# The third pair's cross product in two clusters of column tiles, its codes summed by GpSimd

## The chip, the core and the metric

The kernel runs on one core of one Trainium2 chip, with the core's engines TensorE (matrix products into PSUM), VectorE, ScalarE, GpSimd, and SyncE, which issues most of the DMA transfers. The metric is device time in microseconds, lower is better. Three runs of the kernel before gave 602.71, 602.85 and 603.24 us, median 602.85 us.

## The reference

`x` is 16 sequences of 64 rows by 1024. The layer is a cross product with a quantised context, a causal attention with 32 heads, and a dense layer with low-rank experts, each on the normalised row and added to `x`. Cut to what matters here:

```python
def fake_quant(x, scale, zp):
    q = clip(round(x / scale + zp), 0, 255)
    return (q - zp) * scale

x = x + matmul(fake_quant(layernorm(x)), fake_quant(ctx))     # ctx: (16, 1024, 1024)
h = layernorm(x)
q, k, v = split(h @ qkv_w + qkv_b)                            # rope on q and k, 32 heads of 32
x = x + softmax(rope(q) @ rope(k).T / sqrt(32) + causal) @ v @ out_w + out_b
x = x + layernorm(x) @ W.T + bias + sum_e w_e * (layernorm(x) @ A_e.T) @ Bf_e.T
```

The quantised product is worked out on integer codes: the product of the centred row codes with the raw context codes, a term from the sum of the context codes over the contracted index (times 128 less the zero point of the rows), and a constant per row.

## The kernel before

The 16 sequences are taken two at a time as 128 rows: pairs 0 to 7, each first through the cross product, then through attention; a last part does the dense layer for all pairs. While pair i is in attention, the cross product of pair i+1 is done between its matrices. So the stage of this text, "the attention of pair 1", contains the cross product of pair 2, the third pair.

**Context codes.** The context of a pair comes in 16 chunks of 128 by 1024, c0 to c15, 512 KB each. SyncE loads them (`load_chunk`) into three slots in turn (`raw` 0, `raw` 1, `lnt`); the load of chunk c waits until chunk c-3 is coded. ScalarE turns a chunk into codes (`quantise`, line 381) in a ring of eight tiles (`code`), so that chunk c waits until TensorE has read chunk c-8 (semaphore `s_cmm`).

**Two ways to multiply.** A pair below `TILED` (3) is multiplied chunk by chunk (`chunk`, line 1420): two products of 128x512, whose weights hold 64 columns of row codes and 64 columns of ones; the rows of ones give the sum of the codes on TensorE itself. VectorE adds the result to `xb` in four passes over half the partitions (`cross_evac`, lines 966 and 967). A pair from `TILED` on has its chunks loaded in turn from its two sequences (`block_of`), is multiplied with 64-column weights, one sequence on each half of the PE array (`cross`, line 1435), eight chunks in a cluster, and GpSimd sums the codes (`add_codes`, line 826, two integer additions of 128x256 per chunk). VectorE casts the sums to float16 (`sums_as_f16`, line 972), TensorE adds them with eight more products (`cross_shift`, line 1447, which waits for `s_accf` of that cast), and VectorE adds the result to `xb` in two passes over all partitions (`tiled_evac`, line 978).

**Order of work.** There is no scheduler: each engine's program is written by hand, and an engine takes its instructions strictly in that order. TensorE's order in a pair is `next_pair(i, ahead)`: six column blocks of the projections, `qkv(i, 0)` to `qkv(i, 5)`, each of 8 steps of 3 matmuls, with other work hung behind a step by the dictionary `{step: [...]}`: the turns of `q` and `k` (`qk_turn`), the scores (`scores`), the turns of the probabilities (`p_turn`), the values (`values`). Then come `project` and `x_turn` of the next pair. ScalarE and VectorE have a `next_pair` each; the pair 1 runs with `late=True`, for in it the last weights 25 to 31 are split into a high and a low half: `w(j)` is `weight_hi` on ScalarE (line 358) and `weight_lo` on VectorE (line 960), and the high half of weight j waits for the low half of weight j-1 (`s_wlo`).

Of the softmax, `softmax_in` is a maximum and a subtraction (lines 1024 and 1027), ScalarE does `exponent` (417), and `softmax_out` is a sum, a reciprocal and a product (1033 to 1035). `v_evac` (408) takes the values' projection out of PSUM, and `values_due` makes TensorE wait for it.

Of the kernel before, what the change touches and what calls it, by code (L numbers as in the profile page):

```python
# [34 lines left out]
CODE_BASE = 1024.0  # L35
CODE_PAIR = 9.473556003354462e+21
CODE_SUM = -0x20032000
TILED = 3
RAW, RING = 2, 8
VECTOR_CHUNK = CHUNKS - 4  # L40
NEG_RSQRT_MAGIC = 0x5F3759DF - (1 << 22) - (1 << 31)
# [15 lines left out]
def build(nc, x, ctx_in, consts, qkv_w, out_w, bias_rows, out_bias, ffn_wt, ffn_bias, lora_a, lora_b, lora_w, out):  # L57
# [6 lines left out]
    with es:  # L64
# [20 lines left out]
        at = sb("at", [P, 5 * DM], F32)  # L85
# [253 lines left out]
        def _(act):  # L339
# [163 lines left out]
            def next_pair(i, more, late=False):  # L503
                def q(*cs):
                    for c in cs:
                        quantise(i + 1, c)

                def w(j):
                    if late:
                        weight_hi(j)  # L510
                w(25)
                q(2)
                if not late:
                    q(3, 4, 5)
                a_high(i + 1, 0)
                a_high(i + 1, 1)
                if late:
                    q(3, 4)
                    w(26)
                    q(5, 6)  # L520
                    w(27)
                if not late:
                    q(6)
                qk_evac(i, 0)
                q(7)
                if late:
                    q(8)
                w(28)
                qk_evac(i, 1)
                if not late:  # L530
                    q(8)
                q(9)
                w(29)
                if late:
                    q(10, 11)
                exponent(i, 0)
                if not isinstance(i, int) or i < PAIRS - 2:
                    rows_after_next(i)
                q(12 if late else 10)
                exponent(i, 1)  # L540
                qk_evac(i, 2)
                if late:
                    q(13)
                else:
                    q(11, 12)
                p_evac(i, 0)
                if late:
                    p_evac(i, 1)
                    qk_evac(i, 3)
                    w(30)  # L550
                    q(14)
                    w(31)
                    v_evac(i, 0)
                    q(15)
                else:
                    q(13)
                    qk_evac(i, 3)
                    q(14, 15)
                    p_evac(i, 1)
                exponent(i, 2)  # L560
                exponent(i, 3)
                c_high(i, 0)
                p_evac(i, 2)
                if late:
                    v_evac(i, 1)
                p_evac(i, 3)
                if more:
                    quantise(i + 2, 0)
                    quantise(i + 2, 1)
                c_high(i, 1)  # L570
                x_high(i + 1, 0)
                x_high(i + 1, 1)
                if late:
                    value_bias()
# [275 lines left out]
        def _(dve):  # L850
# [269 lines left out]
            def next_pair(i, late=False):  # L1120
                def w(j):
                    if late:
                        weight_lo(j)
                if not late:
                    row_stats(i + 1, x_early)
                row_codes(i + 1, x_early)
                w(25)
                rotate(i, 0)
                w(26)
                out_base(i)  # L1130
                x_shift(i + 1)
                rotate(i, 1)
                w(27)
                w(28)
                softmax_in(i, 0)
                rotate(i, 2)
                softmax_in(i, 1)
                softmax_out(i, 0)
                if late:
                    softmax_out(i, 1)  # L1140
                    rotate(i, 3)
                    w(29)
                else:
                    rotate(i, 3)
                    softmax_out(i, 1)
                if late:
                    cross_evac(i + 1, 0)
                w(30)
                softmax_in(i, 2)
                if not late:  # L1150
                    v_sum(i, 0)
                softmax_in(i, 3)
                w(31)
                if late:
                    softmax_out(i, 2)
                    softmax_out(i, 3)
                    c_low(i, 0)
                    cross_evac(i + 1, 1)
                else:
                    sums_as_f16(i + 1)  # L1160
                    softmax_out(i, 2)
                    softmax_out(i, 3)
                    tiled_evac(i + 1, 0)
                    c_low(i, 0)
                    tiled_evac(i + 1, 1)
                    v_sum(i, 1)
                norm2(i + 1)
                c_low(i, 1)
                x_low(i + 1, 0)
                x_low(i + 1, 1)  # L1170
                out_evac(i, 0)
                out_evac(i, 1)
# [188 lines left out]
        def _(pe):  # L1361
# [376 lines left out]
                project_whole(1, 1, {5: [at(x_turn, 1)]})  # L1738

            def next_pair(i, ahead):  # L1740
                def c(*cs):

                    for n in cs:
                        if ahead:
                            chunk(i + 1, n)

                def t(*ks):

                    if ahead:
                        cross(i + 1, *ks)  # L1750

                def shifted():
                    if ahead:
                        cross_shift(i + 1)

                def m(u):
                    if not ahead:
                        merge(u)

                def codes():  # L1760
                    if ahead:
                        next_codes(i + 1)

                def codes_turned(e):
                    if ahead:
                        pe.wait_ge(s_ah, 2 * i + 3 + e)

                pe.wait_ge(s_xl, 2 * i + 2)
                if isinstance(i, int) and i == 1:
                    qkv(i, 0, {5: [at(next_codes, i + 1)]})  # L1770
                    qkv(i, 1, {0: [at(c, 0)], 2: [at(c, 1)], 4: [at(codes_turned, 0), at(qk_turn, i, 0)], 5: [at(c, 2)], 7: [at(c, 3)]})
                    qkv(i, 2, {1: [at(c, 4)], 3: [at(codes_turned, 1), at(qk_turn, i, 1)], 4: [at(c, 5)], 6: [at(middle_biases, i), at(scores, i, 0)], 7: [at(c, 6)]})
                else:
                    qkv(i, 0)
                    qkv(i, 1, {3: [at(codes)], 5: [at(m, 0)], 6: [at(codes_turned, 0), at(qk_turn, i, 0)]})
                    qkv(i, 2, {4: [at(m, 1), at(codes_turned, 1), at(qk_turn, i, 1)], 6: [at(middle_biases, i), at(scores, i, 0), at(t, 0, 1, 2, 3)]})
                late = isinstance(i, int) and i == 1
                if late:
                    qkv(i, 3, {1: [at(c, 7)], 6: [at(turned, i, 1), at(qk_turn, i, 2)]})
                    qkv(i, 4, {1: [at(turned, i, 2), at(p_turn, i, 0)], 3: [at(p_turn, i, 1)], 4: [at(evacuated, i, 1), at(qk_turn, i, 3)], 6: [at(scores, i, 1)], 7: [at(c, 8, 9)]})  # L1780
                    qkv(i, 5, {1: [at(c, 10, 11)], 2: [at(c, 12, 13)], 3: [at(c, 14, 15), at(values_due, i, 0)], 4: [at(values, i, 0)],
                               6: [at(evacuated, i, 0), at(p_turn, i, 2)], 7: [at(p_turn, i, 3)]})
                else:
                    qkv(i, 3, {2: [at(m, 2)], 6: [at(turned, i, 1), at(qk_turn, i, 2)]})
                    if ahead:
                        qkv(i, 4, {1: [at(turned, i, 2), at(p_turn, i, 0)], 4: [at(qk_turn, i, 3)], 6: [at(scores, i, 1)], 7: [at(p_turn, i, 1)]})
                    else:
                        qkv(i, 4, {1: [at(turned, i, 2), at(p_turn, i, 0), at(m, 3)], 4: [at(qk_turn, i, 3)], 6: [at(scores, i, 1)], 7: [at(p_turn, i, 1)]})
                    qkv(i, 5, {1: [at(m, 4)], 2: [at(m, 5)], 3: [at(values_due, i, 0)], 4: [at(t, 4, 5, 6, 7), at(shifted), at(values, i, 0)],
                               6: [at(evacuated, i, 0), at(p_turn, i, 2)], 7: [at(p_turn, i, 3)]})  # L1790
                project(i, 0, 0, {2: [at(values_due, i, 1)], 3: [at(values, i, 1)]})
                project(i, 1, 0)
                if ahead:
                    x_turn(i + 1)
                else:
                    merge(6)
                    merge(7)
                project(i, 0, 1)
                project(i, 1, 1)
# [133 lines left out]
```

## Time and profile before

| | before |
|---|---|
| median of 3 runs | 602.85 us |
| the profiled execution | 601.86 us |
| its span in the trace | 599.6 us |
| PE busy | 581.1 us, 97% of the span |
| DVE, ACT, POOL busy | 77%, 49%, 22% |
| granted TensorE clock | full speed throughout |

The span runs from the first to the last instruction of the trace; 2.3 us of the profiled execution lie around it. Pair 1's attention runs from 102.8 to 162.7 us of the span, pair 2's from 162.7 to 219.0 us. An engine's busy share says nothing of who waits for whom: for that the waits of the engine with the highest share are read, and then the stretch where the change lies, instruction by instruction.

### The profile page before, as it was taken

Reading aid. Unit: us, or ns where it says so; the run is one execution under the profiler, and the core shown is the slowest. Engines: PE = TensorE matmul, PEld = TensorE weight load, DVE = VectorE, ACT = ScalarE, POOL = GpSimd, SP = SyncE. Lnnn points to the kernel's source line nnn. Section 1 sums busy time; section 2 is a strip of 40 time slices with the busy share of each in tenths; the row PEclk is TensorE's granted clock in tenths of the full one; section 3 lists DMA queues with packets and bytes.
Section 4 is the critical chain, followed back from the end, with each engine's and each line's share of the span. In section 5 each row is a group of like instructions: output and inputs, shape, how many; then the busy total and the mean of one; then the engine's idle time right before and its main releaser. Section 6 shows DMA issues by size and latency. Waiting matters only on the chain.

```text
span 599.6 us, 12924 instructions
## 1 busy us (share of the span) xinstructions
PE 581.1 (97%) x4922; PEld 295.5 (49%) x4922; DVE 462.4 (77%) x903; ACT 291.3 (49%) x359; POOL 131.3 (22%) x173
## 2 busy tenths in 40 slices
PE   3899999999999999999999999999999999999998
PEld 1354454455545545554555455455545554444445
DVE  6799997778777866887787878678964789977751
ACT  5878795865456535734464555537330242210100
POOL 4000010000165333713551554336100000000000
PEclk9999999999999999999999999999999999999999
DMA  8999996862365254517451643455331035477531
GB/s 316 388 386 395 398 387 230 262 236 72 127 218 205 87 193 159 215 65 275 149 206 68 247 179 136 142 209 175 105 137 40 1 112 205 124 143 174 146 99 54
DMA packets 53713, 111.82 MB, mean 186 GB/s; under 512 B 18602, under 2 KB 18986, under 8 KB 53680
## 3 DMA queue, kind: packets, MB, share of 16 engines
q1 hardware_dynamic: 37760, 104.35, 49.4%
q10 hardware_dynamic: 15648, 6.48, 5.0%
q0 software_dynamic: 272, 0.55, 0.2%
q8 instruction: 21, 0.34, 0.2%
q14 instruction: 12, 0.10, 0.0%
HBM read 99.30 MB, written 8.39 MB: 180 GB/s over the span
## 4 chain that ended last, share of the span: by engine, by line
PE 87%; DVE 7%; SPq 2%; DMA 2%; issue 1%; ACT 1%; DVEq 0%
PE dense L1375 15%; PE dense L1377 14%; PE dense L1376 14%; PE turn L1366 6%; PE dense L1587 4%; PE dense L1588 4%; PE dense L1845 4%; PE dense L1589 4%; DVE wq L960 4%; PE cross L1435 3%; PE score L1548 3%; PE dense L1603 2%; PE cross L1420 2%; PE dense L1848 2%; SPq L668 2%; PE score L1574 2%
## 5 line engine op out<-in xcount | busy, mean ns | idle before, releaser
L1375 PE MATMUL dense<-wq,xn_h 128*128 128x512 f16 x376 | 142.8, 380 | 0.0
L1376 PE MATMUL dense<-wq,xn_h 128*128 128x512 f16 x376 | 142.5, 379 | 0.0
L1377 PE MATMUL dense<-wq,xn_l 128*128 128x512 f16 x376 | 142.5, 379 | 0.0
L826 POOL TENSOR_TENSOR acc<-code,acc 128x256 int32<-128x256 int32 x140 | 110.0, 815 | 112.2 <-ACT code L381 112.2
L381 ACT ACTIVATE code<-raw,cst,qc 128x1024 uint8<-128x1024 f32 x72 | 88.2, 1236 | 9.0 <-DMA raw<-in_ctx 8.6
L381 ACT ACTIVATE code<-lnt,cst,qc 128x1024 uint8<-128x1024 f32 x32 | 39.6, 1239 | 41.4 <-DMA lnt<-in_ctx 27.5
L1377 PEld LDWEIGHTS dense<-wq,xn_l 128*128 128x128 f16 x376 | 36.8, 98 | 44.4
L1375 PEld LDWEIGHTS dense<-wq,xn_h 128*128 128x128 f16 x376 | 36.7, 98 | 40.2 <-issue 3.6
L1376 PEld LDWEIGHTS dense<-wq,xn_h 128*128 128x128 f16 x376 | 36.8, 98 | 35.1
L1587 PE MATMUL dense<-wo,rope 128*128 128x512 f16 x112 | 42.5, 380 | 0.0
L1588 PE MATMUL dense<-wo,rope 128*128 128x512 f16 x112 | 42.4, 379 | 0.0
L1589 PE MATMUL dense<-wo,rope 128*128 128x512 f16 x112 | 42.4, 379 | 0.0
L1021 DVE SCALAR_TENSOR_TENSOR at<-cst,score 128x512 f32<-128x512 f16 x24 | 16.4, 682 | 33.3 <-PE score L1548 33.3
L417 ACT ACTIVATE at<-at 128x512 f32<-128x512 f32 x32 | 19.9, 624 | 35.5 <-DVE at L1027 35.4
L826 POOL TENSOR_TENSOR acc<-code,lw 128x256 int32<-128x256 int32 x20 | 11.6, 611 | 107.7 <-ACT code L381 107.7
L404 ACT ACTIVATE at<-turn 128x512 f32<-128x512 f32 x32 | 18.9, 592 | 32.5 <-PE turn L1366 23.0
L642 ACT ACTIVATE spare<-lnt 128x1024 f16<-128x1024 f32 x7 | 7.4, 1057 | 52.6 <-DVE lnt L1281 52.6
L1007 DVE TENSOR_TENSOR rope<-dense,cst 128x512 f32<-128x512 f32 x32 | 22.0, 689 | 10.6 <-PE dense L1377 7.7
L423 ACT ACTIVATE at<-turn 128x512 f32<-128x512 f32 x32 | 18.8, 588 | 17.8 <-PE turn L1366 17.7
L1058 DVE SCALAR_TENSOR_TENSOR xa<-dense,xa 128x512 f32<-128x512 f32 x16 | 11.0, 690 | 18.1 <-PE dense L1589 18.0
L1035 DVE TENSOR_TENSOR at<-at,ssum 128x512 f32<-128x512 f32 x32 | 23.5, 734 | 1.1
L1013 DVE TENSOR_TENSOR rope<-rope 128x512 f32<-128x512 f32 x32 | 23.0, 718 | 1.4
(242 smaller groups left out, 1044.7 us busy)
## 6 DMA issues: line engine op xcount, KB each, us to landing
raw<-in_ctx SPq DMA_DIRECT2D x72, 512.0 KB, 4.7
lnt<-in_ctx SPq DMA_DIRECT2D x32, 512.0 KB, 3.4
wo<-in_ctx SPq DMA_DIRECT2D x16, 512.0 KB, 9.5
wo<-in_qkv_w SPq DMA_DIRECT2D x12, 512.0 KB, 11.7
wq<-in_qkv_w SPq DMA_DIRECT2D x8, 512.0 KB, 12.1
x_scratch<-xa SPq DMA_DIRECT2D x8, 512.0 KB, 2.9
wo<-in_out_w SPq DMA_DIRECT2D x7, 512.0 KB, 7.2
wq<-in_ctx SPq DMA_DIRECT2D x6, 512.0 KB, 11.6
```

The costliest lines, as they stand in the source:

```text
L381: act.activation(low_bytes, src, ACT.Identity, scale=qc[:, 1:2], bias=z2).then_inc(s_u8, 2 if isinstance(i, int) and i == 0 and c == VECTO ...
L826: ins = pool.tensor_tensor(sums[:, cols], words[:, cols], acc_from.to_broadcast([P, half]) if c < 2 else sums[:, cols], ALU.add)
L960: dve.scalar_tensor_tensor(lo, staged(j), WSC, hi, ALU.mult, ALU.subtract).then_inc(s_wlo, 1)
L1035: dve.tensor_tensor(p3, p3, ssum[:, g % 2, :].unsqueeze(2).to_broadcast([P, HPG, SEQ]), ALU.mult).then_inc(s_p, 1)
L1366: ins = pe.transpose(bank[:, k * P:(k + 1) * P], src[:, c:c + P], ident)
L1375: pe.matmul(bank[:, :], a_h[:, k, :], w_hi, start=(k == 0 and not started), stop=False)
L1376: pe.matmul(bank[:, :], a_h[:, k, :], w_lo, start=False, stop=False)
L1377: ins = pe.matmul(bank[:, :], a_l[:, k, :], w_hi, start=False, stop=(k == KC - 1 and not last))
L1587: pe.matmul(D[n][:, :], c_h[:, k, :], wo_h[:, k, cols], start=(k == 0), stop=False)
L1588: pe.matmul(D[n][:, :], c_h[:, k, :], wo_l[:, k, cols], start=False, stop=False)
L1589: ins = pe.matmul(D[n][:, :], c_l[:, k, :], wo_h[:, k, cols], start=False, stop=(k == KC - 1))
L1845: pe.matmul(D[0][:, :], yn_h[s][:, k, :], w[:, k, 0:NT], start=(k == 0 and w is wf_h), stop=False)
```

## The change

`TILED` goes from 3 to 2, so that pair 2 is multiplied in column tiles as well: its chunks are loaded in the other order, GpSimd's loop over the pairs starts one earlier, and in the attention of pair 1 the chunks, which stood between the steps of the projections, become two clusters, `t(0, 1, 2, 3)` behind the scores in `qkv(1, 2)` and `t(4, 5, 6, 7)` with `cross_shift` behind step 4 of `qkv(1, 5)`. On ScalarE and VectorE the codes and the weight splits of that pair stand in another order, and VectorE's four `cross_evac` passes are replaced by `sums_as_f16` and two `tiled_evac`. In the changed kernel lines from the first pair's helpers on have a number lower by up to eight.

```diff
--- before.py
+++ after.py
@@ -35,7 +35,7 @@
 CODE_BASE = 1024.0
 CODE_PAIR = 9.473556003354462e+21
 CODE_SUM = -0x20032000
-TILED = 3
+TILED = 2
 RAW, RING = 2, 8
 VECTOR_CHUNK = CHUNKS - 4
 NEG_RSQRT_MAGIC = 0x5F3759DF - (1 << 22) - (1 << 31)
@@ -523,41 +523,39 @@
                     q(6)
                 qk_evac(i, 0)
                 q(7)
-                if late:
-                    q(8)
+                qk_evac(i, 1)
                 w(28)
-                qk_evac(i, 1)
+                q(8)
                 if not late:
-                    q(8)
-                q(9)
-                w(29)
-                if late:
-                    q(10, 11)
+                    q(9)
                 exponent(i, 0)
                 if not isinstance(i, int) or i < PAIRS - 2:
                     rows_after_next(i)
-                q(12 if late else 10)
+                if late:
+                    q(9)
+                    w(29)
+                q(10)
                 exponent(i, 1)
                 qk_evac(i, 2)
                 if late:
-                    q(13)
-                else:
-                    q(11, 12)
-                p_evac(i, 0)
-                if late:
+                    q(11)
+                    p_evac(i, 0)
+                    q(12)
                     p_evac(i, 1)
                     qk_evac(i, 3)
+                    q(13, 14, 15)
                     w(30)
-                    q(14)
-                    w(31)
                     v_evac(i, 0)
-                    q(15)
-                else:
+                else:
+                    q(11, 12)
+                    p_evac(i, 0)
                     q(13)
                     qk_evac(i, 3)
                     q(14, 15)
                     p_evac(i, 1)
                 exponent(i, 2)
+                if late:
+                    w(31)
                 exponent(i, 3)
                 c_high(i, 0)
                 p_evac(i, 2)
@@ -1131,8 +1129,8 @@
                 x_shift(i + 1)
                 rotate(i, 1)
                 w(27)
+                softmax_in(i, 0)
                 w(28)
-                softmax_in(i, 0)
                 rotate(i, 2)
                 softmax_in(i, 1)
                 softmax_out(i, 0)
@@ -1143,19 +1141,19 @@
                 else:
                     rotate(i, 3)
                     softmax_out(i, 1)
-                if late:
-                    cross_evac(i + 1, 0)
-                w(30)
                 softmax_in(i, 2)
                 if not late:
                     v_sum(i, 0)
                 softmax_in(i, 3)
-                w(31)
+                w(30)
                 if late:
                     softmax_out(i, 2)
                     softmax_out(i, 3)
+                    sums_as_f16(i + 1)
+                    w(31)
+                    tiled_evac(i + 1, 0)
                     c_low(i, 0)
-                    cross_evac(i + 1, 1)
+                    tiled_evac(i + 1, 1)
                 else:
                     sums_as_f16(i + 1)
                     softmax_out(i, 2)
@@ -1738,12 +1736,6 @@
                 project_whole(1, 1, {5: [at(x_turn, 1)]})
 
             def next_pair(i, ahead):
-                def c(*cs):
-
-                    for n in cs:
-                        if ahead:
-                            chunk(i + 1, n)
-
                 def t(*ks):
 
                     if ahead:
@@ -1768,17 +1760,17 @@
                 pe.wait_ge(s_xl, 2 * i + 2)
                 if isinstance(i, int) and i == 1:
                     qkv(i, 0, {5: [at(next_codes, i + 1)]})
-                    qkv(i, 1, {0: [at(c, 0)], 2: [at(c, 1)], 4: [at(codes_turned, 0), at(qk_turn, i, 0)], 5: [at(c, 2)], 7: [at(c, 3)]})
-                    qkv(i, 2, {1: [at(c, 4)], 3: [at(codes_turned, 1), at(qk_turn, i, 1)], 4: [at(c, 5)], 6: [at(middle_biases, i), at(scores, i, 0)], 7: [at(c, 6)]})
+                    qkv(i, 1, {6: [at(codes_turned, 0), at(qk_turn, i, 0)]})
+                    qkv(i, 2, {4: [at(codes_turned, 1), at(qk_turn, i, 1)], 6: [at(middle_biases, i), at(scores, i, 0), at(t, 0, 1, 2, 3)]})
                 else:
                     qkv(i, 0)
                     qkv(i, 1, {3: [at(codes)], 5: [at(m, 0)], 6: [at(codes_turned, 0), at(qk_turn, i, 0)]})
                     qkv(i, 2, {4: [at(m, 1), at(codes_turned, 1), at(qk_turn, i, 1)], 6: [at(middle_biases, i), at(scores, i, 0), at(t, 0, 1, 2, 3)]})
                 late = isinstance(i, int) and i == 1
                 if late:
-                    qkv(i, 3, {1: [at(c, 7)], 6: [at(turned, i, 1), at(qk_turn, i, 2)]})
-                    qkv(i, 4, {1: [at(turned, i, 2), at(p_turn, i, 0)], 3: [at(p_turn, i, 1)], 4: [at(evacuated, i, 1), at(qk_turn, i, 3)], 6: [at(scores, i, 1)], 7: [at(c, 8, 9)]})
-                    qkv(i, 5, {1: [at(c, 10, 11)], 2: [at(c, 12, 13)], 3: [at(c, 14, 15), at(values_due, i, 0)], 4: [at(values, i, 0)],
+                    qkv(i, 3, {6: [at(turned, i, 1), at(qk_turn, i, 2)]})
+                    qkv(i, 4, {1: [at(turned, i, 2), at(p_turn, i, 0)], 3: [at(p_turn, i, 1)], 4: [at(evacuated, i, 1), at(qk_turn, i, 3)], 6: [at(scores, i, 1)]})
+                    qkv(i, 5, {3: [at(values_due, i, 0)], 4: [at(t, 4, 5, 6, 7), at(shifted), at(values, i, 0)],
                                6: [at(evacuated, i, 0), at(p_turn, i, 2)], 7: [at(p_turn, i, 3)]})
                 else:
                     qkv(i, 3, {2: [at(m, 2)], 6: [at(turned, i, 1), at(qk_turn, i, 2)]})
```

The order of instructions at three places of pair 1's attention follows. First VectorE from its third and fourth `softmax_in` on (`score` is the scores' bank, `smx` the maxima, `at` holds the probabilities, `wo` the output weights, `acc` GpSimd's sums), before:

```order
L1024 TENSOR_REDUCE smx<-score 128x8
L1027 TENSOR_TENSOR at<-score,smx 128x512
L1024 TENSOR_REDUCE smx<-score 128x8
L1027 TENSOR_TENSOR at<-score,smx 128x512
L960 SCALAR_TENSOR_TENSOR wo<-spare,wo 128x1024
L1033 TENSOR_REDUCE ssum<-at 128x8
L1034 RECIPROCAL ssum<-ssum 128x8
L1035 TENSOR_TENSOR at<-at,ssum 128x512
L1033 TENSOR_REDUCE ssum<-at 128x8
L1034 RECIPROCAL ssum<-ssum 128x8
L1035 TENSOR_TENSOR at<-at,ssum 128x512
```

and now:

```order
L1022 TENSOR_REDUCE smx<-score 128x8
L1025 TENSOR_TENSOR at<-score,smx 128x512
L958 SCALAR_TENSOR_TENSOR wo<-wo 128x1024
L1031 TENSOR_REDUCE ssum<-at 128x8
L1032 RECIPROCAL ssum<-ssum 128x8
L1033 TENSOR_TENSOR at<-at,ssum 128x512
L1031 TENSOR_REDUCE ssum<-at 128x8
L1032 RECIPROCAL ssum<-ssum 128x8
L1033 TENSOR_TENSOR at<-at,ssum 128x512
L970 CAST acc<-acc 128x2048
L958 SCALAR_TENSOR_TENSOR wo<-spare,wo 128x1024
L976 SCALAR_TENSOR_TENSOR xb<-cross,lw,xb 128x512
```

The low half of weight 31 (`wo<-spare,wo`), which stood ahead of the two `softmax_out`, now stands behind them, that of weight 30 stands in its old place, and the cast of the sums comes behind the second `softmax_out`.

TensorE at step 2 to 4 of `qkv(1, 5)`, before (`cross` is the cross product's bank, the `score` row at the end is `values(1, 0)`):

```order
L1420 MATMUL cross<-code,q1t 128x512 x4
L1375 MATMUL dense<-wq,xn_h 128x512
L1376 MATMUL dense<-wq,xn_h 128x512
L1377 MATMUL dense<-wq,xn_l 128x512
L1420 MATMUL cross<-code,q1t 128x512 x4
L1375 MATMUL dense<-wq,xn_h 128x512
L1376 MATMUL dense<-wq,xn_h 128x512
L1377 MATMUL dense<-wq,xn_l 128x512
L1574 MATMUL score<-at 32x64 x32
L1375 MATMUL dense<-wq,xn_h 128x512
```

and now:

```order
L1373 MATMUL dense<-wq,xn_h 128x512
L1374 MATMUL dense<-wq,xn_h 128x512
L1375 MATMUL dense<-wq,xn_l 128x512
L1433 MATMUL cross<-code,q1t 64x512 x16
L1445 MATMUL cross<-acc,lw 64x512 x8
L1572 MATMUL score<-at 32x64 x32
L1373 MATMUL dense<-wq,xn_h 128x512
L1374 MATMUL dense<-wq,xn_h 128x512
```

The chunks between the steps have gone, and the second cluster and `cross_shift` stand ahead of `values(1, 0)`.

ScalarE from its third turn of `q` and `k` to the last exponents (`code` is a chunk's codes, `wo<-wo` and `wo<-spare` the high halves of weights 30 and 31, `at<-dense` is `v_evac`, `at<-at` an exponent), before:

```order
L404 ACTIVATE at<-turn 128x512
L381 ACTIVATE code<-raw,cst,qc 128x1024
L423 ACTIVATE at<-turn 128x512 x2
L404 ACTIVATE at<-turn 128x512
L358 ACTIVATE wo<-wo 128x1024
L381 ACTIVATE code<-lnt,cst,qc 128x1024
L358 ACTIVATE wo<-spare 128x1024
L408 ACTIVATE at<-dense 128x512
L381 ACTIVATE code<-raw,cst,qc 128x1024
```

and now:

```order
L381 ACTIVATE code<-lnt,cst,qc 128x1024
L423 ACTIVATE at<-turn 128x512
L381 ACTIVATE code<-raw,cst,qc 128x1024
L423 ACTIVATE at<-turn 128x512
L404 ACTIVATE at<-turn 128x512
L381 ACTIVATE code<-raw,cst,qc 128x1024
L381 ACTIVATE code<-lnt,cst,qc 128x1024
L381 ACTIVATE code<-raw,cst,qc 128x1024
L358 ACTIVATE wo<-wo 128x1024
L408 ACTIVATE at<-dense 128x512
L417 ACTIVATE at<-at 128x512
L358 ACTIVATE wo<-spare 128x1024
```

The last five chunks are spread between the two turns of the probabilities and behind them, and c13, c14 and c15 stand ahead of the high half of weight 30, `v_evac`, the third exponent, the high half of weight 31 and the fourth exponent.

## Rows read from the trace of the kernel before

**Rows 1.** The page's first part: engine, busy time, share of the span, instructions.

```profile
PE 581.1 (97%) x4922; PEld 295.5 (49%) x4922; DVE 462.4 (77%) x903; ACT 291.3 (49%) x359; POOL 131.3 (22%) x173
```

**Rows 2.** TensorE's waits: line, releaser, us in total, times, longest.

```profile
PE turn L1574 <- ACT at L423: 0.3, 1, 0.3
...
PE cross L1420 <- ACT code L381: 0.2, 1, 0.2
```

**Rows 3.** Timeline of TensorE, pair 1: start, duration, instruction, count.

```profile
122.80 1.16 PE L1548 MATMUL score<-at 32*64 32x64 f32 x64
123.90 0.39 PE L1375 MATMUL dense<-wq,xn_h 128*128 128x512 f16 x1
...
137.55 1.16 PE L1548 MATMUL score<-at 32*64 32x64 f32 x64
...
141.89 1.03 PE L1420 MATMUL cross<-code,q1t 128*128 128x512 f16 x4
142.75 0.38 PE L1375 MATMUL dense<-wq,xn_h 128*128 128x512 f16 x1
...
146.51 0.86 PE L1574 MATMUL score<-at 64*32 64x64 f32 x64
147.30 0.39 PE L1375 MATMUL dense<-wq,xn_h 128*128 128x512 f16 x1
...
156.20 1.04 PE L1366 MATMUL turn<-cst,lnt 128*128 128x128 f32 x8
```

**Rows 4.** Timeline of TensorE, pair 2, around the clusters of pair 3's cross product.

```profile
181.32 1.92 PE L1435 MATMUL cross<-code,q1t 128*64 128x512 f16 x16
183.17 0.39 PE L1375 MATMUL dense<-wq,xn_h 128*128 128x512 f16 x1
...
200.46 1.92 PE L1435 MATMUL cross<-code,q1t 128*64 128x512 f16 x16
202.21 1.03 PE L1447 MATMUL cross<-acc,lw 128*64 128x512 f16 x8
203.17 0.86 PE L1574 MATMUL score<-at 64*32 64x64 f32 x64
```

**Rows 5.** Timeline of ScalarE, pair 1: a code, an exponent, `p_evac`, a high half.

```profile
116.42 1.23 ACT L381 ACTIVATE code<-raw,cst,qc 128x1024 uint8<-128x1024 f32 x1
...
128.76 0.63 ACT L417 ACTIVATE at<-at 128x512 f32<-128x512 f32 x1 [1.39 <-DVE at L1027]
...
132.97 0.60 ACT L423 ACTIVATE at<-turn 128x512 f32<-128x512 f32 x1 [0.65 <-PE turn L1366]
...
136.53 1.05 ACT L358 ACTIVATE wo<-wo 128x1024 f16<-128x1024 f32 x1
```

**Rows 6.** Timeline of VectorE, pair 1 from the third `softmax_in`, and the cast of pair 2.

```profile
138.87 0.69 DVE L1024 TENSOR_REDUCE smx<-score 128x8 f32<-128x512 f32 x1
...
141.53 1.22 DVE L960 SCALAR_TENSOR_TENSOR wo<-spare,wo 128x1024 f16<-128x1024 f32 x1
142.66 0.68 DVE L1033 TENSOR_REDUCE ssum<-at 128x8 f32<-128x512 f32 x1
...
144.22 0.68 DVE L1033 TENSOR_REDUCE ssum<-at 128x8 f32<-128x512 f32 x1
...
155.16 0.81 DVE L950 TENSOR_SCALAR lnt<-xb,mv,nw 128x1024 f32<-128x1024 f32 x1
...
200.83 0.69 DVE L972 CAST acc<-acc 128x2048 f16<-128x2048 uint16 x1
```

**Rows 7.** Timeline of ScalarE, pair 2: chunks 12 and 15, which share a slot.

```profile
190.79 1.23 ACT L381 ACTIVATE code<-raw,cst,qc 128x1024 uint8<-128x1024 f32 x1
...
196.98 1.24 ACT L381 ACTIVATE code<-raw,cst,qc 128x1024 uint8<-128x1024 f32 x1 [1.20 <-DMA raw<-in_ctx]
```

**Rows 8.** Timeline of ScalarE, pair 1: chunk 5, for which it waited.

```profile
104.97 1.23 ACT L381 ACTIVATE code<-lnt,cst,qc 128x1024 uint8<-128x1024 f32 x1
...
112.44 1.24 ACT L381 ACTIVATE code<-lnt,cst,qc 128x1024 uint8<-128x1024 f32 x1 [1.02 <-DMA lnt<-in_ctx]
```

**Rows 9.** Timeline of GpSimd, pair 2: additions, beside VectorE's work.

```profile
173.68 2.56 POOL L826 TENSOR_TENSOR acc<-code,acc 128x256 int32<-128x256 int32 x2 [2.09 <-ACT code L381]
...
198.38 1.41 POOL L826 TENSOR_TENSOR acc<-code,acc 128x256 int32<-128x256 int32 x2 [0.92 <-ACT code L381]
```

More of the change, by code:

```diff
@@ L542, in next_pair @@
                 if late:
-                    q(13)
+                    q(11)
+                    p_evac(i, 0)
+                    q(12)
+                    p_evac(i, 1)
+                    qk_evac(i, 3)
+                    q(13, 14, 15)
+                    w(30)
+                    v_evac(i, 0)
                 else:
                     q(11, 12)
-                p_evac(i, 0)
-                if late:
-                    p_evac(i, 1)
-                    qk_evac(i, 3)
-                    w(30)
-                    q(14)
-                    w(31)
-                    v_evac(i, 0)
-                    q(15)
-                else:
+                    p_evac(i, 0)
                     q(13)
@@ L1145, in next_pair @@
                     softmax_out(i, 1)
-                if late:
-                    cross_evac(i + 1, 0)
-                w(30)
                 softmax_in(i, 2)
@@ L1152, in next_pair @@
                 softmax_in(i, 3)
-                w(31)
+                w(30)
                 if late:
```

## The prediction

> **What bounds the kernel now.** I read the page's busy times first: TensorE works 97% of the span [rows 1]. Then TensorE's own waits, to see whether the rest is waiting: from pair 1 on there are two of 0.2 to 0.3 us [rows 2]. So every microsecond of TensorE's instructions counts, and another engine counts only where it makes TensorE wait. The third view is TensorE's timeline in pair 1, where instruction follows on instruction [rows 3], the fourth the same of pair 2, which already works in the way that pair 1's attention is to take [rows 4]; it gives the durations of what is added. Last, ScalarE and VectorE in the same stretches give the time at which their results are there [rows 5 to 8].
>
> **What TensorE saves.** Two chunks between steps take 142.75 - 141.89 = 0.86 us, so one takes 0.43, and the 16 that go take 6.9 us [rows 3]. Added are a cluster, 183.17 - 181.32 = 1.85 us, a second with what it borders on, 202.21 - 200.46 = 1.75, and the eight products of the sums, 203.17 - 202.21 = 0.96 [rows 4]. Sum: 4.6 us. If nothing waited, TensorE would be through 2.3 us earlier.
>
> **First cluster.** It stands behind the first scores, with six chunks gone ahead of them: the scores start at 122.80 - 6 x 0.43 = 120.2, and the cluster 123.90 - 122.80 = 1.10 later, at 121.3 [rows 3]. It needs code 7, finished at 116.42 + 1.23 = 117.65 [rows 5], since nothing ahead of it on ScalarE is moved. No wait, 3.7 us to spare. The price is that code 8, coded at 117.8 before, can only follow when the cluster has read a tile: c8 to c15 start some 4 us late, and are the reason why ScalarE's order counts from there.
>
> **The second cluster and the sums.** I count from s, the start of the second scores, 137.55 before. Ahead of it eight chunks are gone and a cluster is added: 8 x 0.43 - 1.85 = 1.6 us earlier, s = 135.95. Before, the values came at s + 8.96 (146.51) and the next step at s + 9.75 (147.30) [rows 3]. Without the eight chunks in that stretch (3.45) and with the second cluster, TensorE stands ahead of the sums' products at s + 8.96 - 3.45 + 1.75 = s + 7.25.
>
> These products wait for VectorE's cast, and VectorE takes its queue in order. Behind the scores (1.16, and 0.04 until VectorE starts) it has two `softmax_in` (141.53 - 138.87 = 2.66), the low half of weight 30 (142.66 - 141.53 = 1.13), two `softmax_out` (144.22 - 142.66 = 1.56 each) and the cast (0.69) [rows 6]: s + 1.20 + 2.66 + 1.13 + 3.12 + 0.69 = s + 8.80. This is the floor, with no wait in it: TensorE waits at least 1.55 us of the 2.3 saved. The gain then is at most 0.75.
>
> Two things lie on top. (1) ScalarE's high half of weight 31 waits for the low half of weight 30 on VectorE, and the fourth exponent is queued behind it. The low half starts at s + 3.86 and takes 1.22; then the high half 1.05 (0.96 to the next), the exponent 0.63 [rows 5], and the second `softmax_out` starts at s + 5.1 + 1.0 + 0.63 + 0.1 = s + 6.8 instead of s + 6.55. The cast ends at s + 9.05, the products start 0.05 later, the next step comes 0.96 + 0.79 behind, at s + 10.85 = 146.8 against 147.30: gain 0.5. (2) Chunk 15 stands ahead of the high half of weight 30 on ScalarE. It shares a slot with c12, which follows `p_evac` of the first turn: 132.97 before, 1.6 earlier now, so at 131.4; with 0.5 for `p_evac` and 1.23 for the code c12 is done at 133.1 [rows 5]. In pair 2 from the end of c12 (190.79 + 1.23 = 192.02) to the start of c15 (196.98) it took 4.96 us, a wait for the DMA [rows 7]. So c15 starts at about 138.05, its codes take 1.14 to the next, the high half 1.05: the low half on VectorE starts at 140.3, or s + 4.35 instead of s + 3.86. With that delay of 0.5 the gain is 0.05; with a transfer that is in time it stays 0.5. I take a delay of 0.3, nearer to the row. `v_evac`, behind that high half, is ready at 140.75, when TensorE has got to `values_due` (s + 4.75 = 140.7): nothing to pay there yet.
>
> **GpSimd beside VectorE.** GpSimd adds c14 and c15 while VectorE works on weight 30. The trace before has no GpSimd work beside a low half of a weight. The nearest row is a chunk's pair of additions, 1.41 us when alone and 2.56 beside VectorE's addition of two SBUF operands [rows 9]: the engines do hold each other up. Bounds for the low half: 0, and one addition, 1.41 / 2 = 0.7. I take 0.25, since who loses depends on who starts first. The same delay may fall on `rotate` and on the first `softmax_out`; TensorE comes for these more than 1 us after they are ready, so I cost them at nothing. GpSimd itself is done with c15 some 1.5 us after its code, by 141, while the cast starts at s + 8.4 = 144.3 at the earliest. Not late.
>
> The Trainium skill, SBUF — State Buffer, section "Who interferes with whom", says more: a VectorE instruction with two SBUF inputs and a GpSimd instruction that reads SBUF exclude each other for the whole instruction, whoever starts first. The stretched pair of rows 9 agrees with it. By that rule alone the low half of weight 30 loses up to a whole addition, which is the third case below.
>
> **The tail.** VectorE's four half passes give way to two whole ones, but behind the cast nothing is late: before, the normalised row was ready at 155.97 for a turn at 156.20 [rows 3, 6], and with the evacuation begun from about 146.1 the row comes some 2 us earlier. From pair 2 on nothing changes on any engine, and TensorE does not wait there, so a shift of pair 1's end is carried to the end in full. c0 and c1 are now summed at 98 to 100.5 us beside the second normalisation of pair 1, whose row is ready shortly before its turn; bounds 0 and 0.5 us, and I take 0.1.
>
> **Sum.** -6.9 + 4.6 = -2.3; wait for the cast +1.55 (floor), +0.25 (exponent behind weight 31), +0.3 (c15), +0.25 (GpSimd beside the low half), +0.1 (the row of pair 1): +0.15 us on the profiled execution's 601.86, which is its span of 599.6 and 2.3 around it, so 602.0. The median of the runs lies 1.0 above the profiled execution: 602.85 + 0.15 = 603.0 us. What this measurement can tell from no change is 0.2%, 1.2 us.
>
> **Rivals.**
> A. *The saving comes through.* If the sums were cast before TensorE gets to them, the whole 2.3 us would be gained: 600.6. For it: TensorE is the bound, and pair 2 has this cluster with no wait [rows 2, 4]. Against: in VectorE's queue the cast stands behind both `softmax_out`, and the floor above has no wait to lose. Chance 6%.
> B. *The transfer of chunk 15 is late (slower).* Place: c15 ahead of weight 30's high half, `v_evac`, and both exponents on ScalarE. c5 came 112.44 - 106.20 = 6.2 us after c2 was coded [rows 8], 1.3 more than assumed. Then `values_due` waits too and the cast ends 1.3 us later still: with a whole addition in the way (0.45 more than taken) 603.0 + 1.3 + 0.45 = 604.7. It turns the verdict from a delay of 1.2 us on, that is from some 6 us between c12 and c15. Chance 13%, with other waits of the rearranged ScalarE queue in it.
> C. *The full lock.* The low half loses 0.7 us rather than 0.25, and another step on the way 0.2: 603.0 + 0.45 + 0.2 = 603.6. For it: rows 9; against: GpSimd is idle two thirds of the time. Chance 20%.
> D. The forecast, no change to speak of, 602.4 to 603.4: 61%.
>
> Faster by over 0.2% (under 601.65) is A and a bit: 7%. Slower by over 0.2% (over 604.05) is B and the far end of C: 14%. The rest, 79%, is within. The range holds D and C, the floor's gain (602.85 - 0.75 = 602.1) and part of B: 602.0 to 604.2.
>
> **What would show it.** In the profile after: the second cluster in pair 1 at about 141.4, and the sums' products (line 1445) only at about 145 to 146, with a wait on VectorE's cast (line 970) of 1.6 to 2.8 us in TensorE's waits; the values at 146 to 147; the low half of weight 30 started by ScalarE's high half; c15 with a wait for the DMA. TensorE's busy time should be less by some 2.3 us at an unchanged span. I am wrong if line 1445 does not wait (A), if TensorE waits in other places of pair 1, such as the turns or the first cluster, or if pair 2 or later begins to wait.

## The result

The change makes the kernel slower. In the first comparison the changed kernel took 605.45 us in the median of seven executions, the kernel before 602.71. One of the seven took 1508.88 us; without it the median is 605.1, and the ratio, which leaves it out, is 1.0041, with a 95% interval of 1.0030 to 1.0051. In the second, with more executions, it was 604.77 against 602.58, a ratio of 1.0029 (1.0018 to 1.0041). 603.0 us had been forecast, with 604.2 as the upper end of the range and 14% for a slowdown that can be measured.

The first part of the page of the changed kernel, which answers to [rows 1]:

```profile
PE 580.3 (97%) x4930; PEld 294.2 (49%) x4930; DVE 463.6 (77%) x902; ACT 291.4 (48%) x359; POOL 161.0 (27%) x205
```

TensorE works 0.8 us less than before, not 2.3 us less, and the span of this execution is 601.4 us against 599.6. In the stage that the change rearranges, from the turn of pair 1's normalised row to that of pair 2's, it works 53.98 us for 55.95, that is 2.0 less; in this profile it works some 1.2 us more outside the stage, 0.7 ahead of it and 0.6 behind it, where TensorE's order is unaltered. Why is open. TensorE's waits (line, releaser, us in total, times, longest), to be held against [rows 2]:

```profile
PE cross L1445 <- DVE acc L970: 2.3, 1, 2.3
...
PE turn L1364 <- DVE rope L1011: 0.7, 1, 0.7
...
PE turn L1572 <- ACT at L423: 0.3, 1, 0.3
```

Two waits are new. The first was forecast, the second not. They lie in pair 1, as its timeline on TensorE shows (start, duration, instruction, count, in brackets the idle time before it):

```profile
118.73 0.63 PE L1364 MATMUL turn<-cst,rope 128*128 128x128 f32 x4 [0.71 <-DVE rope L1011]
...
121.23 1.16 PE L1546 MATMUL score<-at 32*64 32x64 f32 x64
122.32 1.92 PE L1433 MATMUL cross<-code,q1t 128*64 128x512 f16 x16
...
136.97 1.16 PE L1546 MATMUL score<-at 32*64 32x64 f32 x64
...
142.47 1.92 PE L1433 MATMUL cross<-code,q1t 128*64 128x512 f16 x16
146.70 1.05 PE L1445 MATMUL cross<-acc,lw 128*64 128x512 f16 x8 [2.31 <-DVE acc L970]
147.68 0.86 PE L1572 MATMUL score<-at 64*32 64x64 f32 x64
...
157.37 1.04 PE L1364 MATMUL turn<-cst,lnt 128*128 128x128 f32 x8
```

The values that stood at 146.51 now stand at 147.68, and the turn of pair 2's row at 157.37 instead of 156.20 [rows 3].

**The profiled execution is not the typical one.** It took 603.65 us at a mean granted TensorE clock of 1.0. Of the 15 executions of this kernel in both comparisons ten had a mean clock of 0.997 and took 604.55 to 606.07 us; the five at 0.999 or 1.0 took 603.33 to 604.55. All executions of the kernel before in the two groups of experiments were at 0.999 or 1.0. A second profile of the same kernel (label e1) caught such an execution; it is read with the first experiment.

### The profile page after: what moved, and what is told of

Same layout as the page of the kernel before. It is cut to its first block, busy times and chain, and to the rows that moved or that the text cites. A ratio compares the mean times of both kernels' runs of the same rounds, so it can differ in the third digit from the quotient of the medians.

```text
span 601.4 us, 13009 instructions
## 1 busy us (share of the span) xinstructions
PE 580.3 (97%) x4930; PEld 294.2 (49%) x4930; DVE 463.6 (77%) x902; ACT 291.4 (48%) x359; POOL 161.0 (27%) x205
## 4 chain that ended last, share of the span: by engine, by line
PE 85%; DVE 6%; SPq 4%; DMA 2%; issue 1%; ACT 1%; DVEq 0%; ACTq 0%
PE dense L1373 14%; PE dense L1375 14%; PE dense L1374 14%; PE turn L1364 6%; PE dense L1585 4%; PE dense L1587 4%; PE dense L1586 4%; PE dense L1837 4%; PE cross L1433 3%; PE score L1546 3%; PE dense L1601 2%; DVE wq L958 2%; SPq L666 2%; DMA wq<-in_qkv_w 2%; PE dense L1840 2%; PE score L1572 2%
## 5 line engine op out<-in xcount | busy, mean ns | idle before, releaser
L824 POOL TENSOR_TENSOR acc<-code,acc 128x256 int32<-128x256 int32 x168 | 136.5, 841 | 125.6 <-ACT code L381 125.5
L824 POOL TENSOR_TENSOR acc<-code,lw 128x256 int32<-128x256 int32 x24 | 14.8, 649 | 66.4 <-ACT code L381 66.4
```

The source lines that it names most:

```text
L824: ins = pool.tensor_tensor(sums[:, cols], words[:, cols], acc_from.to_broadcast([P, half]) if c < 2 else sums[:, cols], ALU.add)
```

## The experiments

To compare stages without what happens before and after, I use one measure beside the times: the time in the profile from the turn of pair 1's normalised row (at 100.21 in the kernel before) to that of pair 2's (156.20), which encloses the change. It was 56.0 us before and 57.0 us in the changed kernel's first profile.

**e1: the changed kernel again,** as the yardstick and for a second profile.

> The changed kernel unaltered, as the yardstick of this group. Its profiled execution took 603.65 us at a mean granted clock of 1.0, five of its timed executions 604.55 to 605.62, four of them at a mean clock of 0.997. Theory T1: TensorE's wait of 2.3 us for VectorE's cast in pair 1 makes the chip grant the lower clock for a while afterwards in most executions: 605 us, most executions at 0.997, and if this one's profile has such a stretch, it begins shortly behind the wait. Rival T2: the lower clock comes by chance or at another place: the profile shows it elsewhere, or the share of executions is another.

604.77 us in the median of nine, six of them at 0.997 (604.55 to 606.07, median 605.1) and three at 0.999 or 1.0 (603.33, 603.38, 603.88). The profiled one is of the first kind. TensorE in five stretches of it (stretch, its length, busy time and count of instructions, granted clock, DMA share, GB/s), with the wait for the cast from 144.9 to 147.2:

```profile
143.00:147.00 4.00, 1.88 (x17) 1.00 0.19 78
147.00:148.00 1.00, 0.81 (x8) 0.96 0.00 0
148.00:151.00 3.00, 3.00 (x71) 0.50 0.02 5
151.00:152.00 1.00, 1.00 (x6) 0.83 0.00 0
152.00:155.00 3.00, 3.00 (x19) 1.00 0.00 0
```

and the same in the first profile, where the wait was as long and the clock stayed:

```profile
146.00:147.00 1.00, 0.30 (x4) 1.00 0.00 0
147.00:150.00 3.00, 3.00 (x81) 1.00 0.00 0
150.00:151.00 1.00, 1.00 (x9) 1.00 0.00 0
```

Here one reads where the time goes. Under 1 us after TensorE resumes, the granted clock is 0.50, that is 1.2 instead of 2.4 GHz, and stays there for about 3.4 us; then it is whole again. The matmuls in it follow at 0.43 us instead of 0.22:

```profile
147.19 1.23 PE L1445 MATMUL cross<-acc,lw 128*64 128x512 f16 x8 [2.30 <-DVE acc L970]
148.35 1.19 PE L1572 MATMUL score<-at 64*32 64x64 f32 x64
149.47 0.61 PE L1373 MATMUL dense<-wq,xn_h 128*128 128x512 f16 x1
149.86 0.63 PE L1374 MATMUL dense<-wq,xn_h 128*128 128x512 f16 x1
150.29 0.63 PE L1375 MATMUL dense<-wq,xn_l 128*128 128x512 f16 x1
```

The clock withheld in the stretches adds up to 0.04 + 3 x 0.50 + 0.17 = 1.7 us, and between the medians of the two kinds of execution lie 605.1 - 603.4 = 1.7 us. The stage itself lost a little less: 58.4 against 57.0 us, so 1.4, with the two waits equally long in both profiles. Not everything in it took double the time; from the start of the values to the next step it is 149.47 - 148.35 = 1.12 us instead of 0.79. So the clock cost 1.4 us in the stage, and 1.7 is its upper bound. T1 holds so far; that the wait is the cause is for the next experiments to show.

**e2: the cast first.**

```diff
                 if late:
+                    sums_as_f16(i + 1)
                     softmax_out(i, 2)
                     softmax_out(i, 3)
-                    sums_as_f16(i + 1)
                     w(31)
```

> The cast of the sums stands ahead of both softmax_out of pair 1 instead of behind them. T1: no wait of TensorE ahead of the sums' products in pair 1 (their row starts at about 144.4 us of the span, with no idle time), no lower clock in any execution; 605.4 - 2.3 (wait) - 1.8 (clock) = about 601.2 us. T2 (clock independent of the wait): 605.4 - 2.3 = 603.1 with most executions still at 0.997. Rival T3 (GpSimd beside VectorE and ScalarE's new order cost as much as the wait): TensorE waits for the probabilities instead, and the time stays above 602.7.

601.04 us, ratio to before 0.9974 (0.9963 to 0.9985), no execution below 0.999. Timeline of TensorE at the place:

```profile
142.43 1.92 PE L1433 MATMUL cross<-code,q1t 128*64 128x512 f16 x16
144.18 1.03 PE L1445 MATMUL cross<-acc,lw 128*64 128x512 f16 x8
145.14 0.86 PE L1572 MATMUL score<-at 64*32 64x64 f32 x64
```

No wait between cluster and products, and none in its place: the probabilities, up to 0.6 us later through it, are still there in time. T1's number was 601.2; T2 (603.1) and T3 are out. One line moved makes the change worth having: 3.7 us against e1, of which 2.3 are the wait and most of the rest is the clock.

**e3: the cast between the two `softmax_out`.** The same edit with the cast one line further down.

> The cast stands between the two softmax_out, 1.56 us plus the exponent's wait of 0.17 earlier than in the changed kernel: a wait of 2.31 - 1.73 = 0.6 us. T1: 601.2 + 0.6 = 601.8 us, and whether some executions are at the lower clock tells how long the wait must be for it. T2: 603.7 us with most at 0.997.

601.78 us, ratio 0.9983 (0.9974 to 0.9992), none of 11 executions below a mean clock of 1.0. The wait in its profile:

```profile
PE cross L1445 <- DVE acc L970: 0.5, 1, 0.5
```

A wait of 0.5 us costs about its own length (601.78 - 601.04 = 0.7) and no clock. The profiled execution is the slowest of the eleven, 603.79 us: its stage begins at 101.72 and has near its start a further wait of 0.4 us, for the low part of the normalised row (`xn_l`). That and the wait for the cast are 0.9 of the 1.2 us by which its stage lies above e2's.

**e4: the low half of weight 31 ahead of the cast too.** The edit puts `w(31)` above `sums_as_f16(i + 1)`.

> The low half of weight 31 (1.22 us, 1.14 to the next) stands ahead of the cast too: a wait of 3.45 us. T1: all executions at a lower mean clock, 605.4 + 1.15 = 606.6 us or more. T2: 606.6 us with the same share of executions at 0.997 as the changed kernel.

606.72 us, ratio 1.0063 (1.0043 to 1.0083). A wait of 3.4 us in the profile; five of six executions at 0.997 or lower (one at 0.994), one at 1.0. TensorE's idle time of 0.5, 2.3 and 3.4 us goes with 0 of 11, 10 of 15 and 5 of 6 executions at the lower mean clock. So the slowdown is a matter of chance per execution. That it comes after 2.3 us and not after 0.5 is clear of chance; whether it is likelier after 3.4 than after 2.3, six executions can't tell, and "all executions" was too much. The stage is 59.6 us, 1.1 above e1, which is the longer wait. The median lies 1.95 above e1; the remaining 0.8 lies outside the stage or in executions without a profile, and isn't explained.

**e8: the wait filled.** The cast is as late as in the changed kernel, but TensorE is given 24 products that nobody reads.

```diff
-4: [at(t, 4, 5, 6, 7), at(shifted), at(values, i, 0)],
+4: [at(t, 4, 5, 6, 7), at(constants, 24), at(shifted), at(values, i, 0)],
```

> The changed kernel with 24 products of 128x192 (86 ns each by the row of the 44 that stand before the first pair, 2.1 us), written into a free PSUM bank and read by nobody, between the second cluster and the products of the sums, where TensorE waits 2.3 us. The cast is as late as before. T1 (the idle stretch is what brings the lower clock): mean clock 1.0 in every execution and none at 0.997, 605.0 - 1.7 = 603.3 us. Rival T8 (the clock follows from something else at that place, such as the products of the sums themselves): 605 us, most executions at 0.997.

```profile
143.64 1.92 PE L1433 MATMUL cross<-code,q1t 128*64 128x512 f16 x16
145.49 2.15 PE L1691 MATMUL turn<-cst 128*128 128x192 f16 x24
147.86 1.05 PE L1445 MATMUL cross<-acc,lw 128*64 128x512 f16 x8 [0.22 <-DVE acc L970]
```

All 11 executions were at 0.999 or 1.0. TensorE gets no further than with the wait, and only the clock is saved: that separates idleness from lateness, and T8 falls, for the products of the sums are there as before. The stage measure is 57.0 us, as in the first profile of the changed kernel, against 58.4 in e1. The median, 604.16, is 0.8 us above the expected 603.3, though, and 0.6 below e1. Its executions begin later: in its profile the turn of pair 1's row comes at 101.50, in that of the changed kernel at 100.33, before any edited instruction. That start varies between 100.2 and 101.7 us in the ten profiles, in five of them with a wait of 0.3 to 0.8 us for a softmax result in pair 0. Whether a kernel's layout has a part in that stays open. So e8 shows the cause by the clock and the stage; the price of the clock, 1.4 to 1.7 us, is from e1 and not from e8's median.

**e5: the kernel before, with the additions of pair 2.** GpSimd's loop gets pair 2 in front, its sums are written over by those of pair 3, and the semaphore counts of the ring follow.

```diff
+            for c in range(CHUNKS):
+                add_codes(2, c)
+            pool.wait_ge(s_acc, 2 * CHUNKS)
             with pool.Fori(TILED, PAIRS) as i:
```

> The kernel before with its order and its chunks untouched, but GpSimd adds the codes of pair 2 too, for nothing (the sums are written over by those of pair 3). It prices GpSimd's 16 pairs of additions beside VectorE where TensorE has the old order. Theory T4 (VectorE is stretched as in the changed kernel, 0.4 to 0.5 us per instruction with two SBUF operands that meets an addition, but in the old order the turn of the third block comes 0.6 us after the rotation even so): 602.6 us, no change, no wait of TensorE for the rotation. Rival T5 (GpSimd's additions cost time wherever they are): 603.3 us or more.

602.90 us, ratio 1.0003 (0.9994 to 1.0012), stage 56.0 us as before. VectorE's timeline in it (the low half of weight 26, the sum of rows and bias, the shift of the next rows, and the last step of the rotation of block 1):

```profile
111.97 1.61 DVE L966 SCALAR_TENSOR_TENSOR wo<-wo 128x1024 f16<-128x1024 f32 x1
113.50 1.75 DVE L927 TENSOR_TENSOR xa<-xb,outb 128x1024 f32<-128x1024 f32 x1
115.29 1.11 DVE L938 TENSOR_SCALAR xb<-at,rs 128x1024 f32<-128x1024 f32 x1
...
117.95 0.95 DVE L1019 TENSOR_TENSOR rope<-rope 128x512 f32<-128x512 f32 x1
```

They are as stretched as in the changed kernel and cost nothing, since the rotation is ready at 118.90 for a turn that in this order comes at about 119.8. The median is 0.3 above the 602.6 expected and the interval reaches to where T5 begins, so it is the timeline, with a stage as long as before and no wait for the rotation, by which T4 holds and T5 falls.

**e6: the changed kernel without the sums of pair 2.** GpSimd's loop starts at pair 3, and pair 2's cast and its eight products are left out, with the counts of their semaphores.

> The changed kernel without the sums of pair 2: GpSimd does not add its codes, there is no cast, and the eight products that add the sums to the cross product of pair 2 are left out (so this part of the result is left out); everything else stands as in the changed kernel. Against the kernel with the cast first (601.04 us) it lacks 0.96 us of products and GpSimd's load. T4: the wait of 0.7 us for the rotation of block 1 goes as well: 601.04 - 0.96 - 0.7 = 599.4 us. Rival T6 (the rotation is late because of the new order alone): the wait stays, 600.1 us.

600.36 us, ratio 0.9959 (0.9945 to 0.9972). 599.4 was expected by T4 and 600.1 by T6, so the time alone speaks for T6; the timeline does not. VectorE, the rotation of block 0 and then the same four instructions:

```profile
110.63 0.69 DVE L1015 TENSOR_TENSOR rope<-rope 128x512 f32<-128x512 f32 x1
111.72 1.23 DVE L959 SCALAR_TENSOR_TENSOR wo<-wo 128x1024 f16<-128x1024 f32 x1 [0.40 <-ACT wo L359]
112.86 1.22 DVE L920 TENSOR_TENSOR xa<-xb,outb 128x1024 f32<-128x1024 f32 x1
114.12 0.75 DVE L931 TENSOR_SCALAR xb<-at,rs 128x1024 f32<-128x1024 f32 x1
...
116.42 0.69 DVE L1015 TENSOR_TENSOR rope<-rope 128x512 f32<-128x512 f32 x1
```

None is stretched, the rotation is ready at 117.11, and the turn follows at 118.01 without a wait for it. Cast and products, which e6 lacks too, come more than 20 us later and have no part in this. The stage measure is 52.8 us against 54.6 in e2: 1.8 us, for which 0.96 + 0.7 = 1.7 was forecast. In the medians only 0.7 of it shows; the profiled execution took 599.60 and the others up to 600.56. That difference outside the stage I can't explain.

**e7: the cast first, and the turn of block 1 one step later.**

```diff
-qkv(i, 2, {4: [at(codes_turned, 1), at(qk_turn, i, 1)], 6: [...]})
+qkv(i, 2, {5: [at(codes_turned, 1), at(qk_turn, i, 1)], 6: [...]})
```

> The kernel with the cast first, and the second turn of pair 1 (block 1 of qkv) one step later, behind step 5 instead of 4 of the third block, 0.65 us. T4: the wait of 0.7 us for the rotation goes, the scores behind step 6 still find their evacuation done (needed at about 120.0 us, ready at 119.95): 601.04 - 0.6 = 600.4 us. Rival T7 (the wait only moves, to the scores' evacuation on ScalarE): 601.0 us, with a wait ahead of the scores of pair 1.

600.85 us, ratio 0.9967 (0.9955 to 0.9979), the fastest complete kernel here; the stage measure is 53.95 us, 0.66 less than e2.

```profile
118.80 0.38 PE L1375 MATMUL dense<-wq,xn_l 128*128 128x512 f16 x1
119.25 0.63 PE L1364 MATMUL turn<-cst,rope 128*128 128x128 f32 x4
...
120.45 0.39 PE L1386 MATMUL dense<-bias_t,pick 32*128 32x512 f16 x2
```

Of the wait 119.25 - 118.80 - 0.22 = 0.2 us is left, and the scores do not wait: T4's way, not T7's. The time alone, between T4's 600.4 and T7's 601.0, would not have said so. The median is 0.2 us under e2's and the intervals overlap, so the gain is shown in the stage and not in the time.

| kernel | median us | ratio (95%) | stage us | idle for the cast | mean clock under 0.999 |
|---|---|---|---|---|---|
| changed (e1) | 604.77 | 1.0018 to 1.0041 | 58.4 (first profile 57.0) | 2.3 | 6 of 9 |
| e2 cast first | 601.04 | 0.9963 to 0.9985 | 54.6 | 0 | 0 of 7 |
| e3 cast between | 601.78 | 0.9974 to 0.9992 | 55.8 | 0.5 | 0 of 11 |
| e4 cast later | 606.72 | 1.0043 to 1.0083 | 59.6 | 3.4 | 5 of 6 |
| e5 before, with sums | 602.90 | 0.9994 to 1.0012 | 56.0 | none | 0 of 11 |
| e6 no sums | 600.36 | 0.9945 to 0.9972 | 52.8 | none | 0 of 5 |
| e7 and turn later | 600.85 | 0.9955 to 0.9979 | 53.95 | 0 | 0 of 6 |
| e8 wait filled | 604.16 | 1.0011 to 1.0029 | 57.0 | 0.2 | 0 of 11 |

## Why the prediction was wrong

**TensorE's saving: right, at most a little too large.** 2.3 us were forecast. From e7, which has a wait of 0.2 left, to the kernel before the stage differs by 2.04 us, so some 2.2 without that; the changed kernel's first profile gives 2.0.

**First cluster: right.** No wait for its codes; it started at 122.32 for 121.3, mostly because of the wait for the rotation ahead of it. Code 8 was ScalarE's first late one, at 123.03 behind a wait of 1.6 us for the cluster.

**The wait for the cast: right to 0.05 us, and part of that is luck.** Forecast 1.55 + 0.25 + 0.3 + 0.25 = 2.35, measured 2.31. The floor of 1.55 was worked out soundly; the three terms on top erred both ways and cancelled. VectorE's timeline from the low half of weight 30 to the cast, against [rows 6]:

```profile
140.82 1.75 DVE L958 SCALAR_TENSOR_TENSOR wo<-wo 128x1024 f16<-128x1024 f32 x1
142.50 0.67 DVE L1031 TENSOR_REDUCE ssum<-at 128x8 f32<-128x512 f32 x1
...
144.30 0.69 DVE L1031 TENSOR_REDUCE ssum<-at 128x8 f32<-128x512 f32 x1 [0.17 <-ACT at L417]
...
145.86 0.69 DVE L970 CAST acc<-acc 128x2048 f16<-128x2048 uint16 x1
```

The low half lost 0.53 us beside GpSimd (forecast 0.25, rival C 0.7), and the exponent held the second `softmax_out` 0.17 (0.25). For chunk 15 there was no wait at all: ScalarE coded c13 to c15 without a gap, where 0.3 was forecast.

```profile
135.95 1.23 ACT L381 ACTIVATE code<-raw,cst,qc 128x1024 uint8<-128x1024 f32 x1
137.08 1.23 ACT L381 ACTIVATE code<-lnt,cst,qc 128x1024 uint8<-128x1024 f32 x1
138.21 1.23 ACT L381 ACTIVATE code<-raw,cst,qc 128x1024 uint8<-128x1024 f32 x1
```

c12 was coded at 134.10, 1 us later than reckoned, since the second scores were too (136.97 for 135.95); c15 followed its end by 4.1 us, right behind c14, so this transfer took less than the 4.96 us of pair 2 [rows 7]. Rival B, the late transfer, did not come about. It named the right side, but the time above its threshold is from elsewhere.

**The first step that failed** is the sentence that GpSimd's hold on `rotate` costs "nothing", since TensorE comes "more than 1 us after they are ready". I had weighed the stretching of one rotation step at a time, and not the queue ahead of it. The slack was short of that even without GpSimd's load, 118.01 - 117.11 = 0.9 us in e6. In VectorE's order five instructions that are stretched beside GpSimd stand up to the point at which the rotation of block 1 is ready:

```profile
110.48 1.11 DVE L1011 TENSOR_TENSOR rope<-rope 128x512 f32<-128x512 f32 x1
111.57 1.69 DVE L958 SCALAR_TENSOR_TENSOR wo<-wo 128x1024 f16<-128x1024 f32 x1
113.18 1.75 DVE L919 TENSOR_TENSOR xa<-xb,outb 128x1024 f32<-128x1024 f32 x1
114.97 1.11 DVE L930 TENSOR_SCALAR xb<-at,rs 128x1024 f32<-128x1024 f32 x1
...
117.49 1.09 DVE L1011 TENSOR_TENSOR rope<-rope 128x512 f32<-128x512 f32 x1
```

Against e6 each is 0.36 to 0.53 us longer, 2.2 in all, of which idle time of VectorE takes up some. They delay the end of the rotation from 117.11 to 118.58, and the turn, which the change had brought forward from 119.25 to 118.02, waits 0.71 us. e5 (same load, old order) and e6 (new order, no load) each alone have no such wait: it takes both, the lost slack and the load. By the Trainium skill, SBUF — State Buffer, section "Who interferes with whom", a VectorE instruction with two SBUF inputs, or in a mode that uses two ports, needs an interface that it shares with a GpSimd instruction that reads SBUF, and whichever of the two starts first blocks the other for its whole length. The sizes agree with that: one addition takes 0.7 us alone (1.41 / 2 [rows 9]), and no instruction lost more. e6 against the changed kernel shows the stretching for four forms; the lock itself no run here separates from other ways of sharing.

**The second step that failed** is that a wait was priced at its length. The sum took the 2.3 us idle as 2.3 us, but in ten executions of 15 the clock went down after it, for another 1.4 to 1.7 us. No term and no rival stood for it, although the wait itself was forecast almost exactly. This and not the 0.7 us took the time out of the range: the executions at the full clock, 603.3 to 604.6, would mostly have been in it. e2, e3 and e8 show the cause, e8 most directly. The Trainium skill, TensorE: Matmul & The Clock Gate, section "HAM oscillation — how this bites in real kernels", describes waits of TensorE that bring the lower clock. The trace agrees in kind, with 1.2 GHz for 3.4 us after a wait of 2.3 us; the waits of the page's example are longer, and here the measurement decides.

**The sum, then,** for the typical execution: -2.2 (work) + 2.3 (cast) + 0.7 (rotation) + 1.4 (clock, as the stage shows it) = +2.2 us, or +2.5 with the 1.7 of the medians; measured 604.77 - 602.58 = +2.2 in the second comparison, and 605.1 - 602.7 = +2.4 in the first. From the turn of pair 2's row to that of pair 7's the profiles differ by up to 0.6 us (346.15 before, 346.2 to 346.8 in the others), e6 among the longest, so this has nothing to do with the added sums; its cause stays open.

The term on the normalised row of pair 1 (0.1) was not to be seen: it was stretched to 100.16, and its turn at 100.33 did not wait.

## What to carry to other kernels

Where a queue is strict, a conversion that the bound engine waits for belongs ahead of work whose reader comes later: moving the cast past two softmax steps was worth 3.7 us, and turned a slowdown of 0.3 to 0.4% into a gain of 0.26%. Price a wait of TensorE as long as the one here, 2.3 us, at its length and the clock behind it, here 1.4 to 1.7 us in two executions of three. If it can't be removed, it can be filled: that kept the clock in all 11 executions of e8, but took only 0.6 us off the median, and the kernel stayed 0.2% slower than before. And when work goes to GpSimd, add up the stretching of every VectorE instruction in the queue ahead of the next hand-over, together with the slack that the change takes away there.

## What the runs showed of the hardware

A single idle stretch of 2.3 us, after more than 80 us in which TensorE's waits were at most 0.8 us each, was enough for the clock of 1.2 GHz in ten of 15 executions of one and the same kernel; after 0.5 us it came in none of 11. It stood right behind a cluster in column tiles; what the same idle stretch does in another place no run here shows. And 16 matmuls of 128x512 in halves of the array take 1.85 us [rows 4], where 8 whole ones take 8 x 0.43 / 2 = 1.72 [rows 3], so 0.1 more.
